# A four-place ring for the second layer's weights, their casts at other times, trailing halves ahead of a combination, and a last output in two pieces

## The reference

```python
x = x + xattn(layernorm(x), ctx)      # 8 heads, context (8, 2048, 384)
x = x + attn(layernorm(x))            # causal logits, softmax over the queries' axis
h  = relu(layernorm(x) @ w1.T + b1)   # w1 is (2048, 512)
hq = float_quantize(h, 4, 3)          # 8-bit float
wq = float_quantize(w2, 4, 3)         # w2 is (512, 2048), 8-bit float too
out = float_quantize(hq @ wq.T + float_quantize(b2, 5, 10), 5, 10)
x = x + out
```

## Time and profile before

| | before |
|---|---|
| runs, us | 941.69, 939.42, 939.48 (median 939.48) |
| profiled execution, its own time | 938.56 us |
| its span | 936.8 us |
| TensorE (PE) busy | 917.5 us, 98% of the span |
| VectorE (DVE) busy | 569.3 us, 61% |
| ScalarE (ACT) busy | 607.6 us, 65% |
| GpSimd (POOL) busy | 495.6 us, 53% |
| DMA moved | 122.14 MB, mean 130 GB/s |
| granted TensorE clock | full in all 40 slices |

### The profile page before, as it was taken

The page is one execution under the profiler, slowest core; times in us unless marked ns, Lnnn a source line. Parts: engine busy times, 40 slices in busy tenths (PEclk is TensorE's granted clock), DMA queues, the critical chain, the costliest instruction groups (busy, mean ns, idle before and its releaser), DMA issues.

```text
span 936.8 us, 19453 instructions
## 1 busy us (share of the span) xinstructions
PE 917.5 (98%) x7372; PEld 572.4 (61%) x7372; DVE 569.3 (61%) x985; ACT 607.6 (65%) x1140; POOL 495.6 (53%) x379
## 2 busy tenths in 40 slices
PE   6999999999999999999999999999999999999988
PEld 3666666666666666666666666666665545544433
DVE  7756555665555655556655566556677785485533
ACT  4567777777777777777777777777667142254620
POOL 3356655655666666565566666886777471210000
PEclk9999999999999999999999999999999999999999
DMA  9357777866767677677756678869965331215132
GB/s 317 121 108 141 130 149 145 150 134 130 147 136 136 131 141 135 149 145 149 136 130 142 136 136 164 186 116 186 157 143 112 91 90 45 46 46 115 67 101 78
DMA packets 321915, 122.14 MB, mean 130 GB/s; under 512 B 298657, under 2 KB 298657, under 8 KB 321825
## 3 DMA queue, kind: packets, MB, share of 16 engines
q1 hardware_dynamic: 306832, 92.07, 53.0%
q10 hardware_dynamic: 14992, 28.84, 9.4%
HBM read 45.36 MB, written 2.10 MB: 51 GB/s over the span
## 4 chain that ended last, share of the span: by engine, by line
PE 95%; DMA 2%; DVE 1%; ACT 1%; issue 1%; ACTq 0%; SPq 0%
PE v_ps L561 28%; PE k_ps L561 27%; PE e_ps L561 11%; PE e_ps L609 10%; PE o_ps L631 6%; PE o_ps L634 3%; PE e_ps L853 3%; PE o_ps L652 2%; PE e_ps L847 1%; DMA w_raw<-in_w_t 1%; PE o_ps L847 1%; PE v_ps L774 1%; PE v_ps L847 1%; PE o_ps L783 1%; PE e_ps L644 1%
## 5 line engine op out<-in xcount | busy, mean ns | idle before, releaser
L1685 POOL TENSOR_TENSOR p_l<-p_f,p_h 128x1024 f16<-128x1024 f32 x128 | 272.4, 2129 | 233.7 <-ACT p_f L995 233.7
L993 ACT ACTIVATE p_h<-e_ps,bias 128x512 f16<-128x512 f32 x256 | 175.9, 687 | 4.9 <-POOL p_l L1685 2.4
L995 ACT ACTIVATE p_f<-e_ps,bias 128x512 f32<-128x512 f32 x256 | 176.7, 690 | 0.0
L1285 DVE TENSOR_TENSOR k_l<-k_ps,k_h 128x512 f16<-128x512 f32 x128 | 88.5, 691 | 143.7 <-ACT k_h L967 143.7
L1277 DVE TENSOR_TENSOR v<-v_ps,v 128x512 f16<-128x512 f32 x128 | 88.8, 694 | 119.7 <-ACT v L959 119.7
L1290 DVE TENSOR_REDUCE q_max<-e_ps 128x2 f32<-128x1024 f32 x128 | 150.8, 1219 | 8.2 <-PE e_ps L609 0.2
L561 PE MATMUL v_ps<-wv_h,ctx_h 128*128 128x256 f16 x768 | 126.3, 273 | 0.2 <-DVE v L1277 0.2
L561 PE MATMUL v_ps<-wv_l,ctx_h 128*128 128x256 f16 x768 | 125.7, 273 | 0.0
L561 PE MATMUL v_ps<-wv_h,ctx_l 128*128 128x256 f16 x768 | 125.7, 273 | 0.0
L1677 POOL TENSOR_TENSOR ctx_l<-raw,ctx_h 128x1536 f16<-128x1536 f32 x32 | 99.2, 3101 | 15.4 <-ACT ctx_h L948 14.8
L631 PE MATMUL o_ps<-v,pt_h 128*128 128x130 f16 x1024 | 106.0, 220 | 0.7 <-issue 0.7
(11 more groups left out here) (243 smaller groups left out, 1302.4 us busy)
## 6 DMA issues: line engine op xcount, KB each, us to landing
raw<-in_ctx_t ACTq DMA_DIRECT2D x26, 768.0 KB, 5.4
w_raw<-in_w_t SPq DMA_DIRECT2D x32, 256.0 KB, 2.9
raw<-in_ctx_t SPq DMA_DIRECT2D x6, 768.0 KB, 4.8
pt_h<-p_h SPq DMA_TRANSPOSE x128, 3.4
pt_l<-p_l SPq DMA_TRANSPOSE x128, 3.2
out<-xr SPq DMA_DIRECT2D x8, 256.0 KB, 2.0
x_in<-in_x ACTq DMA_DIRECT2D x6, 256.0 KB, 8.9
o_all<-in_x ACTq DMA_DIRECT2D x6, 256.0 KB, 4.5
```

What stands on the lines that cost most here:

```text
L993: act.activation(p_h[:, s % H_RING, h, :], e_ps[s % 2][:, h, :], ACT.Exp, scale=EXP_SCALE, bias=bias[:, n % 2, h, q:q + 1]).then_inc(p_hi, 1)
L995: act.activation(p_f[:, s % F_RING, h, :], e_ps[s % 2][:, h, :], ACT.Exp, scale=EXP_SCALE, bias=bias[:, n % 2, h, q:q + 1]).then_inc(p_ful ...
L1285: dve.tensor_tensor(k_l[:, n % 2, cols], k_ps[:, :], k_h[:, n % 2, cols], ALU.subtract).then_inc(k_split, 1)
L1685: pool.tensor_tensor(p_l[:, s % L_RING, :, :], p_f[:, s % F_RING, :, :], p_h[:, s % H_RING, :, :], ALU.subtract).then_inc(p_split, 1)
```

## The change

The ring `w2_raw` gets four places and another home: the 8 KB that `ak_h` and `ak_l`, the key weights of attention, held before (free once `mm2_filled` is 24, for which the first load already waited). Chunks 0 to 3 are loaded ahead of the transposes, 4 to 7 behind them, 8 to 15 behind the first layer's last weights. VectorE casts 0 to 3 before `add_up(1, "C11", 0)`, 4 to 7 at the end of block 1, 8 to 11 between two sums of block 2, 12 and 13 at its end, 14 and 15 behind the first sum of block 3. `turned_low(2, 6)` and `turned_low(2, 7)` go ahead of `combine_tokens(1)`. The output gets three PSUM banks in place of two, and its last row is computed, added and stored in two pieces of 256 columns.

```diff
+W2_RING = 4
...
-        ("w1_raw", [P, 4, DCH, P], F32), ("w2_raw", [P, 2, D], F32), ("y16", [P, 2, D], F16)])
+        ("w1_raw", [P, 4, DCH, P], F32), ("y16", [P, 2, D], F16)])
...
+    ffn2_in, ffn2_in_end = place(nc, ffn2_end, [("w2_raw", [P, W2_RING, D], F32)])
...
-        y_bank = t_bank
+        out_pieces = [(r, slice(0, D)) for r in range(B - 1)] + [(B - 1, slice(0, D // 2)), (B - 1, slice(D // 2, D))]
+        y_bank = t_bank[:3]
...
             def load_w2(i):
-                if i >= 2:
-                    sp.wait_ge(w2_q8, i - 1)
-                sp.dma_start(w2_raw[:, i % 2, :], w2_t[i * P:(i + 1) * P, :]).then_inc(w2_raw_landed[i % 2], 16)
+                if i >= W2_RING:
+                    sp.wait_ge(w2_q8, i - W2_RING + 1)
+                sp.dma_start(w2_raw[:, i % W2_RING, :], w2_t[i * P:(i + 1) * P, :])\
+                    .then_inc(w2_raw_landed[i % W2_RING], 16)
...
-            load_w2(0)
-            load_w2(1)
+            for i in range(W2_RING):
+                load_w2(i)
...
-            load_w2(2)
-            load_w2(3)
+            for i in range(W2_RING, 2 * W2_RING):
+                load_w2(i)
             for j in range(12, 16):
                 load_w1(j)
-            for i in range(4, HC):
+            for i in range(2 * W2_RING, HC):
                 load_w2(i)
-            for r in range(B):
-                sp.wait_ge(y_ready, r + 1)
-                sp.dma_start(out[r], xr[:, r, :]).then_inc(out_stored, 16)
+            for i, (r, cols) in enumerate(out_pieces):
+                sp.wait_ge(y_ready, i + 1)
+                sp.dma_start(out[r, :, cols], xr[:, r, cols]).then_inc(out_stored, 16)
...
-            output_row(0, 0)
-            output_row(1, 1)
+            for n in range(3):
+                output_piece(n)
             pe.wait_ge(h_q8, 2 * HC)
-            for r in range(2, B):
-                pe.wait_ge(y_q16, r - 1)
-                output_row(r, r % 2)
+            for n in range(3, len(out_pieces)):
+                pe.wait_ge(y_q16, n - 2)
+                output_piece(n)
...
                 combine_tokens(0)
-                combine_tokens(1)
                 turned_low(2, 6)
                 turned_low(2, 7)
+                combine_tokens(1)
                 combine_tokens(2)
...
                 for k in range(4):
                     tokens_low(k, 1)
+                for i in range(4):
+                    w2_round(i)
                 add_up(1, "C11", 0)
...
                     weights_low(2, "W12")
-                    w2_round(0)
                 if weights:
                     combine_weights(b + 1)
                 if last:
-                    w2_round(8)
-                    w2_round(9)
+                    w2_round(14)
+                    w2_round(15)
                 add_up(b, "C12", 0)
                 if first:
                     weights_low(2, "S1")
-                    w2_round(1)
                 if weights:
-                    w2_round(4)
-                    w2_round(5)
-                if last:
-                    w2_round(10)
-                    w2_round(11)
+                    for i in range(8, 12):
+                        w2_round(i)
                 add_up(b, "C12", 1)
...
-                if last:
-                    w2_round(12)
-                    w2_round(13)
                 add_up(b, "C22", 0)
...
-                if last:
-                    w2_round(14)
-                    w2_round(15)
                 add_up(b, "C22", 1)
-                if first:
-                    w2_round(2)
-                    w2_round(3)
...
                     add_up(b + 1, "C11", 0)
+                if first:
+                    for i in range(4, 8):
+                        w2_round(i)
                 if weights:
                     weights_low(b + 1, "S3")
                     weights_low(b + 1, "W22")
-                    w2_round(6)
-                    w2_round(7)
+                    w2_round(12)
+                    w2_round(13)
```

More of the change, by code:

```diff
@@ L129, in perceiver_kernel @@
     assert ffn2_end == ctx0_base + 4 * DCH * D * 2
+    ffn2_in, ffn2_in_end = place(nc, ffn2_end, [("w2_raw", [P, W2_RING, D], F32)])
+    assert ffn2_in_end <= late_w_end
     ws_tail, ws_tail_end = place(nc, attn_end, [("ws_l0", [P, 7, 2, 2, P], F16)])
@@ L166, in perceiver_kernel @@
     w1_h, w1_l = ffn1.values()
-    w1_raw, w2_raw, y16 = ffn_in.values()
+    w1_raw, y16 = ffn_in.values()
+    w2_raw = ffn2_in["w2_raw"]
     hq, w2_8 = hidden["hq"], ffn2["w2_8"]
@@ L273, in perceiver_kernel @@
         w1_raw_landed = [sem(f"w1_raw_landed{i}") for i in range(4)]
-        w2_raw_landed = [sem(f"w2_raw_landed{i}") for i in range(2)]
+        w2_raw_landed = [sem(f"w2_raw_landed{i}") for i in range(W2_RING)]
         w1_hi = sem("w1_hi")
@@ L541, in _ @@
                 turn_tokens(k, 1, 1)
-            load_w2(2)
-            load_w2(3)
+            for i in range(W2_RING, 2 * W2_RING):
+                load_w2(i)
             for j in range(12, 16):
                 load_w1(j)
-            for i in range(4, HC):
+            for i in range(2 * W2_RING, HC):
                 load_w2(i)
-            for r in range(B):
-                sp.wait_ge(y_ready, r + 1)
-                sp.dma_start(out[r], xr[:, r, :]).then_inc(out_stored, 16)
-            sp.wait_ge(out_stored, 16 * B)
+            for i, (r, cols) in enumerate(out_pieces):
+                sp.wait_ge(y_ready, i + 1)
+                sp.dma_start(out[r, :, cols], xr[:, r, cols]).then_inc(out_stored, 16)
+            sp.wait_ge(out_stored, 16 * len(out_pieces))
         @block.tensor
@@ L849, in combined_product, with output_piece @@
                 mm.then_inc(prod_filled, 1)
-            def output_row(r, slot):
+            def output_piece(n):
+                r, cols = out_pieces[n]
                 for i in range(HC):
-                    mm = pe.matmul(y_bank[slot], hq[:, i, r, :], w2_8[:, i, :], start=(i == 0), stop=(i == HC - 1))
+                    mm = pe.matmul(y_bank[n % 3][:, cols], hq[:, i, r, :], w2_8[:, i, cols],
+                                   start=(i == 0), stop=(i == HC - 1))
                 mm.then_inc(y_filled, 1)
@@ L1456, in w2_round @@
             def w2_round(i):
-                dve.wait_ge(w2_raw_landed[i % 2], 16 * (i // 2) + 16)
-                dve.tensor_copy(w2_8[:, i, :], w2_raw[:, i % 2, :], saturate=False).then_inc(w2_q8, 1)
+                dve.wait_ge(w2_raw_landed[i % W2_RING], 16 * (i // W2_RING) + 16)
+                dve.tensor_copy(w2_8[:, i, :], w2_raw[:, i % W2_RING, :], saturate=False).then_inc(w2_q8, 1)
             def add_up(b, c, p):
@@ L1640, in _ @@
             dve.wait_ge(b2_ready, 1)
[L1641 to L1646, removed]
+            for n, (r, cols) in enumerate(out_pieces):
+                dve.wait_ge(y_filled, n + 1)
+                dve.tensor_tensor(y16[:, r % 2, cols], y_bank[n % 3][:, cols], b2_row[:, cols], ALU.add).then_inc(y_q16, 1)
+                dve.wait_ge(y_q16, n + 1)
+                dve.tensor_tensor(xr[:, r, cols], xr[:, r, cols], y16[:, r % 2, cols], ALU.add).then_inc(y_ready, 1)
         @block.gpsimd
```

## The result

The changed kernel takes 936.61 us (median of 10, 935.09 to 939.30) against 940.75 for the kernel before on the same chip (median of 10, 939.42 to 941.82). The ratio is 0.9961, 95% interval 0.9947 to 0.9974: 4.1 us by the medians, 2.4 to 5.0 by the interval. The forecast was 4.35, 935.1, in a range from 933.5 to 937.2.

What follows compares the result with a forecast made beforehand. TensorE, busy nearly all the time, was taken as the bound, leaving two stalls and the tail. 3.54 + 0 + 0 - 0.03 + 0.54 + 0.3 = 4.35 us off 939.48 gave about 935.1, range 933.5 to 937.2.

Steps and rivals of the forecast that it cites:

- Part 1: Ring and moved casts: block 3's stalls at products (4,0) and (4,1) go, outputs start earlier, 3.54 us gained.
- The slack of 0.27: In block 3, product (4,0) could start at 898.67, ahead of the 898.94 TensorE needs, so no wait expected.
- rival B: Chunks 8 to 11 load late behind w1 loads, delaying block 2's sum; lateness L comes off the gain; chance 0.08.
- Part 2: turned_low pair first: the 1.25 us stall at hidden product 4 moves to block 1's product (7,0); gain 0.
- Rival A: Moving the turned_low pair pays too: 1.25 us more, 5.6 in all, 933.9; chance 0.18.
- (7,0) starts where it did: Block 1's product (7,0) starts at 859.83 again, held by the last transpose, with a wait of 1.4 us in front.
- Part 3: Three output banks: output matmuls already run without a gap between rows, so the third bank gains nothing.
- Part 4: Last output row in two pieces: 0.54 gained on additions, 0.3 on the last store, 0.03 lost on TensorE.

Runs made afterwards that it cites:

- e2: The ring and moved casts alone, with the old order of combine_tokens(1) and whole output rows in two banks; 936.21 us against 941.14 for the kernel before.
- e8: The changed kernel with the ring of four but the casts at the times of the kernel before; 936.56 us against 941.09 before.
- e3: The kernel before with only turned_low(2, 6) and (2, 7) moved ahead of combine_tokens(1); 940.32 us against 941.14 before, ratio 0.9996.
- e5: The changed kernel with turned_low(2, 6) and (2, 7) back behind combine_tokens(1); 936.35 us against 941.09 for the kernel before.
- e7: e6 with turned_low(2, 6) and (2, 7) back behind combine_tokens(1); 935.45 us against 941.09 for the kernel before.
- e6: The changed kernel with two high-half token transposes moved ahead of the first low half on SP's queue; 934.34 us against 941.09 for the kernel before.
- e4: The kernel before with only the last output row in two pieces and three banks; 940.08 us against 941.14 before, ratio 0.9989.
- e1: The changed kernel again, unaltered; 936.48 us against 941.14 for the kernel before, ratio 0.9958.
- e10: The changed kernel with two PSUM banks for the output in place of three; 935.96 us against 940.98 for the kernel before.
- e9: The changed kernel with the loads of chunks 4 to 7 moved from behind the 16 transposes to behind the 13th; 940.86 us against 940.98 before.

## Why the prediction was right

**Part 1 was right in size and place**: 3.54 forecast, 3.55 in the account above, 3.56 in e2. The slack of 0.27 at products (4,0) and (4,1) held, and none of the moved casts waited. The third round's loads (rival B) were never late, though the landings of w2 went up to 5.2 where 4.5 had been the longest. Rival B was also weighed with a wrong size: the four w1 loads are 256 KB each, a megabyte in all and not each. What I did not see is that the new times matter so little: e8 has the gain with the old ones.

**Part 2 was right**: nothing, because a stall that is removed ahead of another resource's schedule is paid there. e3 and e5 show the zero, e7 against e6 the 1.25 that it is worth once the transposes are early. Rival A named this as the condition, and I gave it a chance of 0.18, rightly for the change as it was. The forecast also said that (7,0) starts where it did. That was too simple: it starts when the last of 16 transposes lands, and this moves from one execution to the next. Apart from the 1.25 of the moved stall, (7,0) was 0.18 late in before, but 0.74, 0.98 and 0.55 in e2, e4 and e5, and 0.55 to 0.76 in e1, e3, e8 and e10, and 1.25 in the first profile of the changed kernel. The profile of before was at the low end, and I took it for the rule. The queue shows where the rest comes from: the issues of the last eight transposes took 10.54 us in before (5.34 and 5.20), and 10.89 to 11.64 in the eight others with the same order. What each took above 10.54 is, within 0.04, what (7,0) is late beyond the 0.18 and the moved 1.25. In all profiles an instruction fetch of a few KB passes through the DMA queues within the same stretch, and the transposes pause somewhere in it; whether one causes the other was not tried.

**Part 3** nothing, e10. **Part 4**: 0.54 + 0.3 - 0.03 forecast, 0.84 in the account. The 128 KB store landed in 1.7, 0.3 less. The Trainium skill, DMA: Bandwidth & Descriptors, section "Anatomy of one DMA — SWDGE (gpsimd) path", has a fit for DMAs issued by GpSimd, by which the two sizes would take an estimated 2.3 and 2.6. The difference agrees, the fixed part is about 0.6 too large for these stores from SP's queue, and the measurement decides.

**The step that was missing is the clock.** I took one longer stall in place of two shorter ones as even. The profile of the changed kernel lost 1.66 us behind its gap of 2.3 us. Four of its ten executions have a mean clock of 0.998 and take 937.2 to 939.3, the six others 935.1 to 937.1. The kernels in whose profiles (7,0) is late by 0.55 or not at all (e5, e6, e7) had a full mean clock in all 18 executions. With e2 (0.74 late) there is no execution in 23 at 0.998 or below; the kernels with the ring and (7,0) late by 1.9 or more (the changed kernel, e1, e8, e10) have 11 in 28. The kernel before, with two stalls of 1.6 in block 3, has 11 in the 57 executions beside the experiments, so lower clocks can't all be put down to (7,0); which of its stalls they follow was not looked at. e9 is the sure case: a gap of 4.9, eleven of eleven. The Trainium skill, TensorE: Matmul & The Clock Gate, section "What's actually happening", says of a kernel's first matmuls that the activity monitor runs free of the kernel, so the same kernel gets a different number of slow ones from run to run. The four of ten would be the same thing behind a gap in the middle; the first profile and e1, one kernel, differ so, but their gaps differ too (2.34 and 1.74), and no run here shows which of the two decides.

The median came out 1.5 above the forecast of 935.1, while before was 1.3 above the 939.48 that I had started from: two of the three runs shown were the fastest two of its ten. The median lies in the range, 0.6 from its upper end; by the difference the forecast did better. Even there the closeness is partly luck: 4.1 stands for anything from 2.4 to 5.0, T gives 3.92 for a profile with the full clock (e1) and 1.64 for the one behind whose gap the clock fell, and the terms that I had left out all lie on the side of less.

## What to carry to other kernels

Before counting a removed stall as a gain, follow the engine to the next thing that it shares with a resource on a clock of its own, here a DMA queue with 16 transposes at 1.3 us each: the stall is paid there until that chain is moved too, and then both edits pay (e3 nothing; e6 gains 1.9 us over e1, and 1.25 over e7). When two small stalls become one long one, look at the granted clock behind it. With a ring that was deep enough the exact place of the casts no longer mattered (e8), and a queue that waits for one item should be given the ready ones first.

## What the hardware showed that I had not expected

The granted clock is not the whole story of the first matmuls: in 13 to 16 us of the changed kernel's profile it is recorded as 1.00 while four matmuls of 512 columns take 1.66 us between starts, twice the 0.86 of later. The same program has it in one execution and not in another (e1: 0.86 from the start).

```profile
12.49 1.02 PE L660 MATMUL v_ps<-xt_h,wq_h 128*128 128x512 f16 x4 [0.78 <-ACT xt_h L941]
13.35 1.03 PE L660 MATMUL k_ps<-xt_h,wq_h 128*128 128x512 f16 x4
```

It costs about 1.6 us (the first eight matmuls take 16.24 - 12.89 = 3.35, and in e1 14.21 - 12.49 = 1.72), two fifths of the gain that was to be measured. Such profiles are best compared over the stretch behind it.
